# Loads of x issued by GpSimd behind its picks, stores by SP, each store held until x has landed four pairs further on

## The reference

```
w = weights[subjects]                       # (128, 128, 128)
out = jnp.einsum('bct,bcd->bdt', x, w)      # per sample: w.T @ x
return x + out                              # (128, 128, 1024) f32
```

## Time and profile before

| | |
|---|---|
| median of 3 runs | 330.6 us (330.27 to 332.64) |
| the profiled execution | 329.79 us |
| its span, first to last instruction | 328.0 us |
| moved by DMA | 134.84 MB, mean 411 GB/s over the span |
| busy: DVE, ACT, PE, POOL | 286.9, 285.0, 250.2, 51.5 us |
| mean granted TensorE clock | 0.962 of full speed |

### The profile page before, as it was taken

How to read it: one execution, slowest core, us unless ns; L and a number is a source line. 1 busy time by engine, 2 the same in 40 slices (tenths; PEclk the granted TensorE clock), 3 DMA queues, 4 the chain that set the end, 5 groups by cost and what they waited for, 6 DMA issues and landing times.

```text
span 328.0 us, 3209 instructions
## 1 busy us (share of the span) xinstructions
PE 250.2 (76%) x1036; PEld 107.7 (33%) x1036; DVE 286.9 (87%) x238; ACT 285.0 (87%) x283; POOL 51.5 (16%) x135
## 2 busy tenths in 40 slices
PE   8868888879877876797784977885978976977640
PEld 3323333323433333342231423332423332433310
DVE  4399999999999998869999399999499999699991
ACT  4289999999999998979999499999499999699791
POOL 1731111111111111101111011111011110000000
PEclk9999999999999999979999799999699999799995
DMA  7999999999999999999999999999999999999566
GB/s 283 424 423 423 429 428 427 430 436 426 425 429 436 429 426 432 438 415 431 431 435 424 421 430 435 425 429 430 424 436 432 429 427 435 414 432 428 241 256 256
DMA packets 13881, 134.84 MB, mean 411 GB/s; under 512 B 1056, under 2 KB 1584, under 8 KB 1584
## 3 DMA queue, kind: packets, MB, share of 16 engines
q1 hardware_dynamic: 9232, 67.64, 49.2%
q10 hardware_dynamic: 4640, 67.12, 47.9%
HBM read 67.64 MB, written 67.11 MB: 411 GB/s over the span
## 4 chain that ended last, share of the span: by engine, by line
DMA 49%; ACT 19%; PE 12%; DVE 9%; issue 4%; POOL 2%; POOLq 1%; ACTq 1%
DMA x_ring<-x 48%; ACT results L214 16%; PE product L231 12%; DVE results L181 8%; ACT results L209 3%; POOL weight_ring L138 2%; DMA weight_halves<-weights 1%; DVE weight_bank L151 1%; POOLq L116 1%; ACTq L195 1%; POOLq L138 0%; DVE weight_halves L146 0%; POOLq L52 0%; ACTq L194 0%; POOLq L132 0%
## 5 line engine op out<-in xcount | busy, mean ns | idle before, releaser
L181 DVE COPY results<-product 32x1024 f32<-32x1024 f32 x231 | 282.2, 1222 | 29.4 <-PE product L231 24.0
L231 PE MATMUL product<-x_ring,weight_ring 64*128 64x512 f32 x1024 | 242.4, 616 | 63.8 <-DVE results L181 25.8
L214 ACT COPY results<-product 32x1024 f32<-32x1024 f32 x217 | 217.6, 1003 | 5.0 <-DVE results L181 2.1
L231 PEld LDWEIGHTS product<-x_ring,weight_ring 64*128 64x128 f32 x1024 | 104.5, 192 | 201.7 <-issue 142.6
L209 ACT COPY results<-product 32x1024 f32<-32x1024 f32 x64 | 64.0, 1000 | 26.7 <-PE product L231 25.5
L138 POOL COPY weight_ring<-weight_bank 64x256 f32 x128 | 50.6, 396 | 216.7 <-PE product L231 204.1
L240 PE MATMUL product<-results 128*128 128x512 f32 x12 | 7.8, 822 | 1.5 <-DVE results L155 1.5
L240 PEld LDWEIGHTS product<-results 128*128 128x128 f32 x12 | 3.1, 271 | 5.3 <-issue 3.9
L187 ACT COPY weight_bank<-weight_halves 64x1024 f32<-64x1024 f32 x1 | 2.0, 2031 | 3.2 <-DVE weight_halves L146 3.2
L151 DVE COPY weight_bank<-weight_halves 64x1024 f32<-64x1024 f32 x3 | 3.2, 1075 | 0.1
L159 DVE TENSOR_SCALAR subject_row<-subject_row 1x128 int32<-1x128 int32 x1 | 0.2, 215 | 2.5 <-DMA subject_row<-subjects 2.5
## 6 DMA issues: line engine op xcount, KB each, us to landing
x_ring<-x SPq DMA_DIRECT2D x32, 2048.0 KB, 36.7
out<-results ACTq DMA_DIRECT2D x32, 2048.0 KB, 11.7
weight_halves<-weights SPq DMA_DIRECT2D x1, 512.0 KB, 4.3
subject_row<-subjects ACTq DMA_DIRECT2D x1, 8.0 KB, 3.2
```

The lines of the kernel that those rows point to most:

```text
L181: last = dve.tensor_copy(target(tile, a, q), rows(tile, a, q))
L214: last = act.copy(target(tile, a, q), rows(tile, a, q))
L231: last = pe.matmul(product[slot % PRODUCTS][a][:, cols], weight_ring[half, slot, r, :], x_ring[half, slot, r, cols], start=r == 0, stop=r ...
```

## The change

The loads of x move from SP to POOL. POOL issues the first four behind the building of the identity, before its first picks; then each load right behind the picks of its own pair, load 4 also after x of pair 0 has landed. The stores move from ACT to SP. SP issues the store of a pair when both engines have copied it and, as long as there is such a pair, when x of the pair four further on has landed (eight tiles, `X_FIRST`). The last four stores have no such wait. SP and no longer ACT waits for all stores at the end. The copies, multiplies, buffers and their sizes stay.

```
+X_FIRST = 4
...
         def _(sp):
             sp.dma_start(weight_halves[:, :, :, :], ...
             for pair in range(PAIRS):
-                lap, place = divmod(pair, PAIR_SLOTS)
-                if lap:
-                    sp.wait_ge(picked, (pair + 1) * PAIR)
-                elif place >= LOADS_AHEAD:
-                    sp.wait_ge(x_in[place - LOADS_AHEAD], DMA_INC)
-                sp.dma_start(x_ring[:, place * PAIR:(place + 1) * PAIR, :, :], x_of_pair[pair]).then_inc(x_in[place], DMA_INC)
+                place = pair % RESULTS
+                sp.wait_ge(act_copied, (pair + 1) * PAIR + PRODUCTS)
+                sp.wait_ge(dve_copied, (pair + 1) * PAIR + PRODUCTS)
+                ahead = pair + X_FIRST
+                if ahead < PAIRS:
+                    sp.wait_ge(x_in[ahead % PAIR_SLOTS], (ahead // PAIR_SLOTS + 1) * DMA_INC)
+                sp.dma_start(out_of_pair[pair], results[:, place, :, :]).then_inc(pair_out[place], DMA_INC)
+            for place in range(RESULTS):
+                sp.wait_ge(pair_out[place], DMA_INC * len(range(place, PAIRS, RESULTS)))
...
         def _(pool):
...
+            def load(pair):
+                place = pair % PAIR_SLOTS
+                pool.dma_start(x_ring[:, place * PAIR:(place + 1) * PAIR, :, :], x_of_pair[pair]).then_inc(x_in[place], DMA_INC)
+
+            for pair in range(LOADS_AHEAD):
+                load(pair)
             pool.wait_ge(clamped, 1)
             for pair in range(PAIRS):
...
                     done.then_inc(picked, 1)
+                if pair >= LOADS_AHEAD:
+                    pool.wait_ge(picked, (pair + 1) * PAIR)
+                    if pair == LOADS_AHEAD:
+                        pool.wait_ge(x_in[0], DMA_INC)
+                    load(pair)
...
         def _(act):
...
-            def store(pair):
-                place = pair % RESULTS
-                act.wait_ge(act_copied, (pair + 1) * PAIR + PRODUCTS)
-                act.wait_ge(dve_copied, (pair + 1) * PAIR + PRODUCTS)
-                act.dma_start(out_of_pair[pair], results[:, place, :, :]).then_inc(pair_out[place], DMA_INC)
...
-                act.copy(target(tile, *blocks[0]), rows(tile, *blocks[0]))
-                if j == 0 and pair:
-                    store(pair - 1)
-                for a, q in blocks[1:]:
+                for a, q in BLOCKS[:ACT_BLOCKS[tile % len(ACT_BLOCKS)]]:
                     last = act.copy(target(tile, a, q), rows(tile, a, q))
                 last.then_inc(act_copied, 1)
-            store(PAIRS - 1)
-            for place in range(RESULTS):
-                act.wait_ge(pair_out[place], DMA_INC * len(range(place, PAIRS, RESULTS)))
```

More of the change, by code:

```diff
@@ L36, in subject_residual_kernel @@
     PAIRS, PAIR_SLOTS = TILES // PAIR, SLOTS // PAIR
-    assert SLOTS % PAIR == 0 and REST % PAIR == 0 and LOADS_AHEAD < PAIR_SLOTS and PAIR * 2 * K == C
+    assert SLOTS % PAIR == 0 and REST % PAIR == 0 and LOADS_AHEAD == X_FIRST == PAIR_SLOTS - 1 and PAIR * 2 * K == C
     BANKS = T // PSUM_BANK_COLS
@@ L207, in _ @@
                     act.wait_ge(pair_out[place], pair // RESULTS * DMA_INC)
-                blocks = BLOCKS[:ACT_BLOCKS[tile % len(ACT_BLOCKS)]]
-                act.copy(target(tile, *blocks[0]), rows(tile, *blocks[0]))
-                if j == 0 and pair:
-                    store(pair - 1)
-                for a, q in blocks[1:]:
+                for a, q in BLOCKS[:ACT_BLOCKS[tile % len(ACT_BLOCKS)]]:
                     last = act.copy(target(tile, a, q), rows(tile, a, q))
                 last.then_inc(act_copied, 1)
-            store(PAIRS - 1)
-            for place in range(RESULTS):
-                act.wait_ge(pair_out[place], DMA_INC * len(range(place, PAIRS, RESULTS)))
         @block.tensor
```

## The result

The changed kernel took 326.24 us (median of 4 runs, 326.17 to 326.55) against 330.71 us for the kernel before; the ratio is 0.9868, with a 95% interval of 0.9821 to 0.9916. Run again beside the experiments it came to 327.1 against 330.04, ratio 0.9902 (0.9869 to 0.9935). So it is faster by 1.0 to 1.3%, and both intervals leave out 1. Forecast were 322.0 us and 2.6%: the sign is right and the time lies inside the range of 319 to 329, but outside the 319 to 324 that had a chance of 0.62, and the gain is half of the forecast one. Medians are of all runs of a kernel; the ratios leave out the few runs in which the chip was in a slower state.

A forecast was written before the change was run, and what follows sets the result against it. Transfers were taken to bound the kernel until x has landed, then copies with stores waiting; minus 9.0 us for holes, plus 0.6 and 0.3, made -8.1 from 329.79, so 321.7, written as 322.0 us; range 319.0 to 329.0.

The forecast's parts named there:

- the rival of a slower queue: Loads on GpSimd's queue move at a lower rate beside SP's stores; 336.5 us with 5% lost, chance 0.12.
- its smaller signs: Among them: stores at 9.8 us intervals, a median store near 8 to 10 us, PE's waits for x behind pair 25.
- The sum: Whole kernel: minus 9.0 us for the end's holes, plus 0.6 and 0.3 us, giving -8.1 us.
- Plus 0.6 us: At the start: the first load is issued by GpSimd at least 0.4 us later, partly covered by the weights.
- Plus 0.3 us: Between x31's landing and store 27's first data: the rest of store 26 covers the delay; bounds 0 to 1.6 us.
- 1.3 us from the last data to the end of the span: At the end, after five stores back to back: 1.3 us, from 319.1 to a span of 320.4.
- 1.8 us between span and execution: Outside the span: profiled execution 329.79 against span 328.0, forecast as 321.7 against 319.9.
- the hole there at 308.0 to 312.5: Near the end of the kernel before: 40 of 428 GB/s moved, so 4.1 us idle, counted as gain.
- Compute's time to spare: At the end: pair 31 copied at 307.6, DMA occupied with stores 27 to 30 until 314.2; 6.6 us to spare.
- The points about GpSimd: GpSimd's issue of a load takes 1 to 2 us, priced at nothing beyond 0.6, as GpSimd idles 204.1 us.
- a dear issue: GpSimd needs 4 us or more per load, so first data and picks come later; 325 us, chance 0.12.
- the gate gives nothing: The gate on stores does not bind, or opens so late that compute stands still; 330 us, chance 0.14.

The follow-up runs named there:

- no_gate: The changed kernel without the wait for x in front of a store; 333.4 us, ratio 1.007 to the kernel before.
- lag_two: The kernel before with each store issued one pair later, no wait for x, queues and engines untouched; 325.98 us, ratio 0.9892.
- one gate off: The changed kernel with only the store of pair 27 no longer waiting for x of pair 31; 326.45 us, ratio 0.9893 to the kernel before.
- the shorter gate: The changed kernel with the store of pair k waiting for x of pair k+2 instead of k+4; 331.01 us, ratio 0.9992 to the kernel before.
- the last gates off: The changed kernel with the stores of pairs 26 and 27 not waiting for x of pairs 30 and 31; 328.6 us, ratio 0.9908 to the kernel before.
- the fastest variant: The changed kernel with loads issued early on ACT's hardware queue and pair 27's store without its wait; 324.11 us, ratio 0.9804 to the kernel before.

## Why the prediction was half right

**The bound and the mechanism: right.** Stores held back bring x31 in earlier, and the tail becomes stores back to back. No holding back, no gain (no_gate); held back in another way, the same gain (lag_two). The forecast had x31 at 294.6 and it came at about 296; it had 24.5 us for five stores, and from 296.5 to 321.0 it was 24.5 us. The middle went at 428 GB/s with the other queue, so the rival of a slower queue did not happen. Three of its smaller signs failed: stores do not follow each other by 9.8 us but by about 7.5 and 12.3 in turn (9.9 in the mean), the median store takes 11.7 us and not 8 to 10, and only two of PE's five waits for x lie behind pair 25. What the Trainium skill (SBUF — State Buffer, the box on the "DVE blocks DMA" trap) says of DMAs issued by GpSimd did not show either: the issues take 713 ns, min and median, and the rate stays at 428 GB/s from 24 to 288 us, with DVE copying for 252.81 of these 264 us. The Trainium skill names fp32 copies from SBUF to SBUF there as what triggers it, and these read PSUM.

**The sum: 8.1 us forecast, 4.0 us of span gained.** Three terms of it were sized too small.
- "Plus 0.6 us" for the start on GpSimd's queue. The first 8 us moved 0.55 MB less (209 against 278 GB/s), 1.3 us; and the whole swap cost 2.3 us by the kernel without a gate. I took the moment of the issue as the price and had no row for how fast such a queue fills at first.
- "Plus 0.3 us" in front of store 27, because the rest of store 26 covers it. The stretch 294.5 to 296.5 moved 82 GB/s, 1.6 us lost: the upper end of the bounds I had given. Store 26 did not cover it, because the landing of x31 waits for the engine that is behind while the other fifteen have finished store 26 too.
- "1.3 us from the last data to the end of the span". The sum left this as it was before, at no change. After 321.0 there are 3.0 us in which about one engine works, the thin end: 1.7 more.

0.7, 1.3 and 1.7 us are 3.7 of the 4.1 by which the span of 324.0 missed 319.9. A fourth term stands outside the span: the forecast kept 1.8 us between span and execution, and the changed kernel needs 2.5 (326.55 less 324.0), 0.7 more, as every run with the loads on GpSimd does. The last two of the three have one cause, and are no two separate gains to be had: with the hole filled (one gate off) the time fell by 0.65 us at most. That cause is the engine that is behind, and the trace of before showed it and I read over it: the hole there at 308.0 to 312.5 is not empty, it moves 40 GB/s at a share of 0.10, one or two engines finishing store 29. I counted it as idle time that can be won back whole.

**Compute's time to spare: 6.6 us forecast, wrong.** I took 13.0 us from x31's landing. With the gate the last loads land 6.8 us apart (289.1 and 295.9), less than a pair's 9.0 us, so the chain runs from x30: copies ended at 313.3, not 307.6. In this kernel it still fits under the stores; with the shorter gate and with the last gates off it is the end and takes the gain away. The points about GpSimd were right: 0.71 us a load is hidden by its 169.0 us of waiting for PE.

Of the single rivals, "a dear issue" is refuted (0.71 us, where 4 were needed) though its 325 us are nearest to the result, and "the gate gives nothing" by the gate's 5.6 to 6.7 us.

## What to carry to other kernels

When loads and stores share a full DMA and the compute is only a little faster, hold stores back by a few tiles, so that the last load lands early and the backlog fills the tail; a store call moved by one pair gave as much here as a new gate on other queues. Then look at the first 8 us after every change of queue, and at the last microseconds: a few us at 30 to 50 GB/s are not idleness, but one DMA engine that is behind, and all that waits for a whole landing waits for it (here x31's last increment came 6.6 us after its first). Size the end of such a pipeline from the last two loads, not the last.

## What the runs showed of the hardware

1500 written-out clears beside a pure stream, with their 12 packets of instructions, cost the transfers 10.7 us, at the end all of it on one of sixteen DMA engines (31 GB/s, share 0.07), although the queue section gives the packets 0.1% of the engines. Whether the packets or the clears do it is not separated. The changed kernel has 8 such packets and the fastest variant ends with 4 us at 53 GB/s; its 324.1 us stand 3.6 us over the floor of 320.5 that the transfers alone reach.

The queue of GpSimd is as fast as SP's once it runs (428 GB/s), but in the first 8 us it moved 180 to 222 GB/s (209 in the changed kernel, 180 without a gate) against 278 to 282 with the loads on SP or ACT, and the execution is 2.5 us longer than its span against 1.8 and 2.1.
